# Attention with relative positions and a routed low-rank layer on one core: the product with the values whole instead of in halves, and the order of the transposed maxima, the wide products and a wait for VectorE

## The reference

```python
# block 1: attention, 16 heads of 16, with a learned bias by distance
q, k, v = heads(lin(ln(x), Wq, bq)), heads(lin(ln(x), Wk, bk)), heads(lin(ln(x), Wv, bv))
rel = rel_emb[arange(L)[None, :] - arange(L)[:, None] + 511]      # past the end: the last row; negative: from the end
qk = einsum('bhld,bhrd->bhlr', q, k) / 4 + einsum('bhld,lrd->bhlr', q, rel)
x = x + ln(lin(softmax(qk) @ v, Wo, bo))
# block 2: base layer, a shared low-rank layer, six routed ones of which two are taken
g = softmax(ln(x) @ router_W.T + router_b); w = its two largest, divided by their sum + 1e-6
x = x + ln(base(ln(x)) + sharedB(sharedA(ln(x))) + sum_e w_e * B_e(A_e(ln(x))))
```

## Time and profile before

| | before |
|---|---|
| median of 3 runs | 6341.79 us |
| the profiled execution | 6342.86 us |
| its span, first to last instruction | 6341.1 us |
| mean granted clock of TensorE | 0.985 of full speed |
| busy: TensorE, its weight loads | 94%, 89% |
| busy: VectorE, GpSimd, ScalarE | 79%, 58%, 49% |
| chain that ended last | TensorE 83%, VectorE 8%, issue 4%, VectorE's queue 3% |
| DMA | 16% of 16 engines |

### The profile page before, as it was taken

How to read it: one execution, slowest core, us unless ns; L and a number is a source line. 1 busy time by engine, 2 the same in 40 slices (tenths; PEclk the granted TensorE clock), 3 DMA queues, 4 the chain that set the end, 5 groups by cost and what they waited for, 6 DMA issues and landing times.

```text
span 6341.1 us, 408511 instructions
## 1 busy us (share of the span) xinstructions
PE 5961.8 (94%) x178176; PEld 5617.6 (89%) x178176; DVE 4987.0 (79%) x10289; ACT 3127.8 (49%) x5145; POOL 3652.9 (58%) x4709
## 2 busy tenths in 40 slices
PE   5999999999999999999999999999999999999997
PEld 4989899899998998898999899899999999998987
DVE  3787788878788887878887888888788788887786
ACT  1555455455555554555555555455555555554554
POOL 5555655565565555555655655555565556556555
PEclk7999999999999999999999999999999999999998
DMA  3111121111212112121121211112111121211211
GB/s 87 39 44 52 36 61 36 54 44 38 60 36 62 36 36 62 36 61 34 42 58 36 60 37 49 47 40 60 36 53 45 36 60 40 59 37 36 62 36 27
DMA packets 570090, 296.74 MB, mean 47 GB/s; under 512 B 384177, under 2 KB 534689, under 8 KB 568625
## 3 DMA queue, kind: packets, MB, share of 16 engines
q1 hardware_dynamic: 568624, 272.86, 16.0%
HBM read 184.46 MB, written 88.60 MB: 43 GB/s over the span
## 4 chain that ended last, share of the span: by engine, by line
PE 83%; DVE 8%; issue 4%; DVEq 3%; POOLq 1%; ACT 1%; POOL 0%; SPq 0%; DMA 0%
PE sc L667 22%; PE pw L693 15%; PE sc L683 14%; PE sc L662 13%; PE pm L714 4%; PE pw L700 4%; PE pw L714 4%; PE pm L674 4%; DVE r L962 3%; DVEq L973 2%; DVE y2n L928 2%; DVE nm L971 1%; PE pm L727 1%; PE pm L705 1%; DVE gate L1005 1%
## 5 line engine op out<-in xcount | busy, mean ns | idle before, releaser
L962 DVE TRANSPOSE_TENSOR_REDUCE r<-sc 128x32 f16<-128x1024 f32 x2048 | 2548.8, 1245 | 52.0 <-PE sc L667 51.4
L667 PE MATMUL sc<-rm,tw 96*128 96x32 f16 x65536 | 2293.4, 177 | 71.6 <-issue 70.8
L847 ACT ACTIVATE prob<-sc 128x1024 f32<-128x1024 f32 x2048 | 2097.3, 1024 | 193.7 <-PE sc L683 141.3
L667 PEld LDWEIGHTS sc<-rm,tw 96*128 96x128 f16 x65536 | 1979.9, 97 | 79.5 <-issue 79.0
L662 PE MATMUL sc<-qm,ks 96*128 96x64 f16 x32768 | 1639.8, 193 | 28.8 <-DMA ks<-qk_s 15.5
L971 DVE TENSOR_REDUCE nm<-pm 16x32 f16<-16x256 f32 x2048 | 840.8, 411 | 753.7 <-PE pm L674 750.3
L662 PEld LDWEIGHTS sc<-qm,ks 96*128 96x128 f16 x32768 | 1302.8, 98 | 34.3 <-issue 34.2
L683 PE MATMUL sc<-nmm,pick 128*128 128x64 f16 x32768 | 1302.0, 193 | 2.5 <-DVE nmm L974 1.2
L683 PEld LDWEIGHTS sc<-nmm,pick 128*128 128x128 f16 x32768 | 1151.9, 98 | 122.4 <-issue 105.5
L693 PE MATMUL pw<-prob,vs 128*32 128x128 f32 x32768 | 1115.7, 277 | 129.8 <-DVE nm L971 124.7
L693 PEld LDWEIGHTS pw<-prob,vs 128*32 128x32 f32 x32768 | 842.6, 110 | 185.8 <-DVE nm L971 137.4
(11 more groups left out here) (131 smaller groups left out, 5803.9 us busy)
## 6 DMA issues: line engine op xcount, KB each, us to landing
raw<-qk_s SPq DMA_DIRECT2D x774, 64.0 KB, 2.8
tw<-tw_s SPq DMA_DIRECT2D x512, 72.0 KB, 2.1
v_s<-vpad SPq DMA_DIRECT2D x136, 256.0 KB, 3.6
vs<-v_s SPq DMA_DIRECT2D x64, 512.0 KB, 3.7
ks<-qk_s SPq DMA_DIRECT2D x384, 64.0 KB, 2.5
xin<-x SPq DMA_DIRECT2D x138, 128.0 KB, 2.9
qk_s<-qkh SPq DMA_DIRECT2D x272, 64.0 KB, 1.7
qk_s<-qkl SPq DMA_DIRECT2D x272, 64.0 KB, 1.6
```

The source lines that it names most:

```text
L667: last = mm(out3[:, :, 2 * k:2 * k + 2], tw[:, jp, u:u + P], rm[:, i, k, :, :], start=False, stop=False, skip_group_check=True)
L847: A(prob[:, jp % 2, :, :, i * IW:(i + 1) * IW], sc[:, 2 * buf:2 * buf + 2, :].rearrange("p c (h i) -> p c h i", i=IW), ACT.Exp).then_inc(s ...
L962: v.tensor_reduce(r1[:, 0:2 * H], sc[:, 2 * buf:2 * buf + 2, :].rearrange("p c (h i) -> p (c h) i", i=IW), axis=AX.X, op=ALU.max, apply_tr ...
```

## The change

The product with the values of a pair is issued whole at k = 1, where its first half stood, and no product stands at k = 2. The maxima of the step before are transposed ahead of the first half of the scores at k = 2 and, while there are tiles to project, at g = 5; elsewhere they keep their place. The wide product stands ahead of the wait for VectorE's reduction in every step, and the wait is left out in steps that have no small product. No instruction is added or taken away apart from those waits.

```diff
+MIXED = (0, 3, 8, 10, 11, 12)
...
-            def pv(jp, half):
+            def pv(jp):
-                for col in (2 * half, 2 * half + 1):
+                for col in range(4):
                     for c in range(2):
                         for q in range(4):
                             h = 4 * col + q
...
-                        pv(pj, 0)
-                    elif k == 2:
-                        pv(pj, 1).then_inc(s_pv, 1)
-                    else:
+                        pv(pj).then_inc(s_pv, 1)
+                    elif k == 3:
                         transpose_parts(t * NJP + jp - 1)
...
                     old = a if g == 0 else att
+                    early = k == 2 or (g == 5 and proj)
+                    if early:
+                        if read is not None:
+                            pe.wait_ge(*read)
+                        if old:
+                            transpose_max(t * NG + g)
...
                         scores(g, 0, buffer(ph, g))
-                    if read is not None:
-                        pe.wait_ge(*read)
-                    if old:
-                        transpose_max(t * NG + g)
+                    if not early:
+                        if read is not None:
+                            pe.wait_ge(*read)
+                        if old:
+                            transpose_max(t * NG + g)
                     if att:
                         scores(g, 1, buffer(ph, g)).then_inc(s_scores, 1)
-                    wide_first = k == 1 or g in (0, 8)
-                    if wide_first:
-                        wide(t, n, g, att, proj, a)
-                    if old:
+                    wide(t, n, g, att, proj, a)
+                    if old and (k == 1 or g in MIXED):
                         pe.wait_ge(s_nmr, t * NG + g)
                     read = mixed(t, g, att, a, b)
-                    if not wide_first:
-                        wide(t, n, g, att, proj, a)
                     if old:
                         shift(buffer(ph, g - 1), t * NG + g)
```

## The result

The changed kernel takes 6411.93 us in the median (6407.89 to 6415.29, 4 runs) against 6343.09 (6341.11 to 6353.11) of the kernel before: a ratio of 1.0106, 95% interval 1.0094 to 1.0119. It is slower by 69 us where 13 were forecast; 6356 was the number, 6268 to 6445 the range.

A forecast was written before the change was run, and what follows sets the result against it. TensorE's own work plus its few waits was taken to set the time. Losses of 2.40 less gains of 2.37 us a tile, with restarts 0.1, gave 13 us over 128 tiles: 6356 us, range 6268 to 6445.

The forecast's parts named there:

- restarts: TensorE loading weights anew after each of nine short waits, some 0.01 us each, bringing the loss to 0.1 a tile.
- (a): Product with the values issued in one go: 0.23 us saved a pair, 0.92 a tile.
- (b): TensorE's waits for `nm` at steps 6 and 15 go: 1.45 us a tile saved.
- (e): Step 6: gate on VectorE runs later, its comparison no longer held by GpSimd; the shift waits 0.40 us.
- (c): Transposition at k = 3 waits for maxima the second half product had covered: 0.98 us a tile lost.
- (d): Early transposition at step 5 waits for maxima delayed by `nmm` meeting GpSimd's weighting: 0.60 us a tile lost.
- (f): Step 15: shift waits for `nmm` behind `y2n`, with GpSimd's mask taken as out of the way: 0.27 us lost.
- (g): Step 0: shift waits for `nmm`, with no late wait before it: 0.15 us lost.
- 128 * 0.1: Last step of the sum: 0.1 us lost in each of 128 tiles, 13 us in all.
- A: Rival: early transposition at step 5 doesn't wait, so (d) goes and (e) shrinks: 6279 us; chance 0.27 with shorter waits.
- B: Rival: normalisation `xn1` on VectorE is held by GpSimd's mask, 0.9 to 1.0 us a tile: 6475 us; chance 0.15.
- C: Rival: the waits simply go with nothing in their place, 303 us saved: 6040 us; chance 0.03.

The follow-up runs named there:

- experiment 3: Kernel before with only the wide products moved ahead of the wait; product with the values in halves, no early transposition: ratio 0.9914 to the kernel before.
- experiment 1: Changed kernel with the early transposition at step 5 taken back, kept at k = 2 alone: ratio 1.0106 to the kernel before.
- experiment 5: Changed kernel with GpSimd's weighting also waiting until VectorE's multiplication `nmm` of step 4 is done: ratio 1.046 to the kernel before.
- experiment 6: Six tiles instead of three in the loop's body: changed kernel 0.9995, experiment 3 0.982, both to the kernel before.
- experiment 8: Query loads issued later: in experiment 3 plus early transpositions at k = 2 0.9988, changed kernel 1.0107, six-tile experiment 3 0.9824, to the kernel before.

## Why the prediction was right or wrong

The places of the waits were right; the size was a fifth of what came, since the forecast was a small difference of two sums. That the direction was right owes something to luck: the sum was 0.03 us a tile, 0.07 of the 0.1 are a term for restarts that no run shows, and the bounds of single terms lie 0.8 us and more apart. So does the number's place. 6412 is outside the forecast's own 6325 to 6385; it falls into 6400 to 6450, which had a chance of 0.05 and a reason, the hold of the comparison kept, that did not come.

- **(a) the joined product**: taken 0.23 us a pair. Against experiment 3, which has the same order with halves, the pairs 9+10 and 13+14 are 0.20 and 0.19 shorter. Right. In the pair 1+2 only 0.10: the early transposition at step 2 is followed by its scores after 0.23 us (3044.28 to 3044.51) instead of 0.11. The step of the sum that counted four equal pairs was off by 0.13 there.
- **(b) the waits at steps 6 and 15**: both went, as said. Taken together with what comes back, 5+6 with the joined product is 0.99 us shorter; (a) 0.23 and step 6's part of (b), some 0.95, less (e) 0.40 made 0.78. The 0.21 more is in the prediction's favour and hides part of what follows.
- **(c) the transposition at k = 3**: taken 0.40 at steps 3 and 15, 0.13 at 11, 0.05 at 7. Step 3 is 0.40 longer than with halves (3.04 against 2.64), step 15 0.31, step 11 0.27, step 7 as long. The mechanism is shown by experiment 3: with the second half in its place line 675 waits once in the whole kernel. Step 11 was mis-sized by 0.14; presumably the small product of step 10 covers less of the maxima than was taken, which no run isolates.
- **(d) the early transposition at step 5**: taken 0.60, measured 0.59 (step 4, 3.24 to 3.83; 0.64 against experiments 1 and 3). Right in size, and experiment 1 shows that undoing it gives nothing, because (e) takes it over. That the two are one wait was not said.
- **(e), (f)**: the hold of the comparison fell away (1115 to 198 ns) as walked in (e), and `y2n` is free of the mask (877 to 381) as taken in (f). The waits that were left for the shift were taken as 0.3 to 0.4 at step 6 and 0.27 at step 15; its weight loads wait 0.40 and 0.29. The Trainium skill, page "SBUF — State Buffer", section "Who interferes with whom", has a VectorE instruction with two inputs in SBUF contend with a GpSimd instruction that reads SBUF. The trace agrees here too: in experiment 5 the comparison meets `qkl` again and takes 1.15 us.
- **(g) and step 7**: taken 0.15 at step 0 (0.11 measured; the shift's weight loads wait 0.16) and, in (c), 0.05 at step 7. Step 7 has 0.22, step 8 0.08, and they have it in experiment 3 too. So it comes from the order, not from the joined product: with `nmr` no longer awaited ahead of the transpositions, the shift waits for `nmm`. I counted this only at step 0. That is 0.25 us a tile, the largest miss in the middle tile.
- **The restarts**: 0.07 a tile taken. No run shows this term.

So the middle tile paid 0.20 in the mean and 0.27 by medians where 0.10 was summed, 26 to 35 us for 13: steps 7 and 8 cost 0.25 more than was taken, 11 and 1+2 0.13 each, and 5+6 gave back 0.21 more. **The step that failed is the last one, "128 * 0.1"**: it multiplied the undisturbed tile by all tiles. A third of the tiles lie behind the jump and a third ahead of it, their surplus grew by some 30 to 38 us, and the prediction had no term for it though the row of issue waits was there (70.8 us before, now 87.4, with 13.2 and now 25.8 at the first scores). Experiment 6 shows the surplus to belong to the jump, and the table of gaps shows where it grew: 12 us ahead of the first scores, with the wide products first, and 20 us at step 3, with the joined product and the early transposition together. The mechanism of either is not shown; experiment 8 makes the loads of the queries a part of the second at most.

Of the rivals, A and C fell with the waits at line 675, 0.35 us at step 5 in the tile shown. B did not come: `xn1` (`xn<-x` at lines 928 and 930) takes 377 ns in the mean in both kernels.

## What to carry to other kernels

A long product that is cut in pieces may be cut because each piece covers something: before joining, name for each piece what runs beneath it on the other engines. Here 0.1 to 0.2 us a pair were gained at the cuts, and 0.3 to 0.4 lost beneath three of the four second halves. Two edits made together can hide each other: wide products ahead of a wait alone gave 0.9%, and were buried under the joined product. A walk through one undisturbed tile says what the steady part does; the tiles at a loop's jump need their own term, and unrolling further shows at once how much they hold. A mean clock near 1 can hide short stretches at the lower level that sit in one place: look at the clock in that place.

## What was not expected of the hardware

- A wait of 1.8 us on TensorE is followed by 4 us at a mean granted clock of 0.57 in the tile of experiment 5 shown, and the run's mean falls to 0.952. In the kernel before the clock falls to the lower level too behind 19 of 41 gaps of 1.0 to 1.8 us at the jump (the 19 are 1.2 us and longer), and behind none of the waits of up to 1.06 us at step 6. So the longer waits had a price above their length: in experiment 5 the shift's 0.3 and step 7's 0.6 us are 0.9 a tile, and the measured 1.046 is above the expected 1.032 by 0.7 a tile.
- The jump back of the loop costs TensorE 2.6 us in the tile behind it and 0.4 in the one ahead, 3.1 and 0.8 in the changed kernel, though the loop is built with `hint_back_edge=True`. Halving the jumps gave 0.9 to 1.1%, at least as much as the best reordering here.
- Transpositions of 0.1 us placed ahead of the scores at k = 2 cost 1.0% with the product in halves, 0.32 of the 0.49 us in the middle tile through gaps of issue at the step behind. With the product joined the same placing gained 1.3%. The cause of the gaps is open.
